# A second feed-forward over tokens sorted by expert, instead of all tokens through all experts

## The reference

```python
gates = softmax(x @ Wg)                       # x: 2048 tokens x 128; 8 experts
top_g, top_i = top_k(gates, 2)                # two experts a token
top_g = top_g / top_g.sum(-1, keepdims=True)
w = zeros(2048, 8).at[arange(2048)[:, None], top_i].add(top_g)
gate_h = silu(einsum('td,edf->etf', x, W1))   # 128 -> 256, for each expert
up = einsum('td,edf->etf', x, W3)
y = einsum('etf,efd->etd', gate_h * up, W2)   # 256 -> 128
out = einsum('te,etd->td', w, y)
x = layernorm(x + out)
```

## Time and profile before

| | |
|---|---|
| Median of 3 runs | 1080.46 us |
| Lowest and highest of the runs | 1079.54 and 1086.42 us |
| Span of the profiled execution (first to last instruction) | 1083.5 us |
| Time of the profiled execution around its span | not listed |
| PE busy | 961.3 us, 89% |
| DVE busy | 749.5 us, 69% |
| ACT busy | 562.8 us, 52% |
| POOL busy | 354.1 us, 33% |

### The profile page before, as it was taken

The page is one execution under the profiler, slowest core; times in us unless marked ns, Lnnn a source line. Parts: engine busy times, 40 slices in busy tenths (PEclk is TensorE's granted clock), DMA queues, the critical chain, the costliest instruction groups (busy, mean ns, idle before and its releaser), DMA issues.

```text
span 1083.5 us, 17979 instructions
## 1 busy us (share of the span) xinstructions
PE 961.3 (89%) x6128; PEld 464.6 (43%) x6135; DVE 749.5 (69%) x1554; ACT 562.8 (52%) x621; POOL 354.1 (33%) x744
## 2 busy tenths in 40 slices
PE   5799999999999875799857889999999889999996
PEld 3222223223223543599724333333333335666664
DVE  7689999999997687244445977777778225654456
ACT  4479889888987322122216035455655665322232
POOL 2164345345335300478815013333333431000000
PEclk9599999999999998899955689999999989999999
DMA  5201101100200412267535221122201300001001
GB/s 199 98 2 44 45 1 44 44 24 19 83 1 2 137 29 54 61 160 189 97 88 199 94 90 46 50 86 90 73 17 44 104 2 1 1 15 44 1 1 40
DMA packets 49837, 65.45 MB, mean 60 GB/s; under 512 B 7800, under 2 KB 37848, under 8 KB 46296
## 3 DMA queue, kind: packets, MB, share of 16 engines
q1 hardware_dynamic: 43280, 58.63, 17.4%
q0 software_dynamic: 5632, 4.46, 2.9%
q10 hardware_dynamic: 864, 1.57, 0.4%
HBM read 51.74 MB, written 12.91 MB: 60 GB/s over the span
## 4 chain that ended last, share of the span: by engine, by line
PE 62%; DVE 23%; issue 7%; ACT 4%; DMA 2%; POOL 1%; DVEq 0%; SPq 0%; ACTq 0%
PE causal_ps L1243 10%; PE acc_ps L769 9%; DVE mx L518 6%; PE acc_ps L1111 6%; PE tail_ps L1057 5%; PE tail_ps L1258 5%; DVE R L1609 4%; PE causal_ps L1094 4%; PE causal_ps L967 3%; DVE tails L1615 3%; PE causal_ps L731 3%; PE tail_ps L967 2%; PE acc_ps L977 2%; PE causal_ps L742 2%; ACT EX L1476 2%
## 5 line engine op out<-in xcount | busy, mean ns | idle before, releaser
L1476 ACT ACTIVATE EX<-causal_ps 128x1024 f32<-128x1024 f32 (+1 forms) x160 | 147.0, 938 | 146.7 <-PE causal_ps L1094 145.5
L518 DVE TENSOR_REDUCE mx<-tail_ps 128x1 f32<-128x512 f32 x266 | 157.4, 633 | 39.2 <-PE tail_ps L1060 21.4
L1335 ACT ACTIVATE R<-R 128x2048 f32<-128x2048 f32 (+1 forms) x80 | 134.7, 1737 | 0.5 <-DVE R L1609 0.5
L1243 PE MATMUL causal_ps<-XT,w 128*128 128x512 f32 x256 | 115.7, 594 | 1.0 <-DVE hid_f L2033 1.0
L1094 PE MATMUL causal_ps<-QE,KE 75*128 75x512 bf16 (+3 forms) x384 | 102.6, 338 | 10.9 <-ACT EX L1476 5.5
L1057 PE MATMUL tail_ps<-KM,QM 72*128 72x512 bf16 (+1 forms) x320 | 102.2, 346 | 8.8 <-DVE mx L518 3.0
L1609 DVE TENSOR_SCALAR R<-causal_ps 128x1024 f32<-128x1024 f32 (+1 forms) x88 | 93.9, 1069 | 14.8 <-PE causal_ps L731 13.7
L1342 ACT ACTIVATE R<-R 128x1792 f32<-128x1792 f32 (+4 forms) x80 | 100.5, 1268 | 0.0
L1615 DVE TENSOR_REDUCE tails<-causal_ps 128x1 f32<-128x768 f32 (+4 forms) x96 | 92.8, 967 | 10.6 <-PE causal_ps L742 9.9
L1517 ACT ACTIVATE act_f<-causal_ps 128x512 f32<-128x512 f32 x64 | 38.1, 597 | 119.2 <-PE causal_ps L1243 119.2
L2262 POOL TENSOR_TENSOR pacer<-eps_ln 128x1 f32<-128x1 f32 x160 | 31.3, 196 | 210.0 <-ACT EX L1476 209.3
(11 more groups left out here) (306 smaller groups left out, 1618.9 us busy)
## 6 DMA issues: line engine op xcount, KB each, us to landing
QS<-q_parts SPq DMA_DIRECT2D x8, 576.0 KB
KS<-k_parts SPq DMA_DIRECT2D x24, 192.0 KB
QM<-q_parts SPq DMA_DIRECT2D x8, 576.0 KB
KM<-k_parts SPq DMA_DIRECT2D x24, 192.0 KB
QE<-q_parts SPq DMA_DIRECT2D x8, 576.0 KB
KE<-k_parts SPq DMA_DIRECT2D x24, 192.0 KB
wg<-in_wg_t SPq DMA_DIRECT2D x16, 256.0 KB
wu<-in_wu_t SPq DMA_DIRECT2D x16, 256.0 KB
```

The lines of the kernel that those rows point to most:

```text
L518: return reduce(mx[:, par, hh, o0:o0 + step * (cnt - 1) + 1:step], scores[:, 0:cnt * w].rearrange("p (c w) -> p c w", w=w), AX.X, op, **how)
L1243: mm = pe.matmul(banks[2 * m + o], w[:, k, m * P:(m + 1) * P], XT[:, n * BANK:(n + 1) * BANK], start=True, stop=True)
L1335: act.activation(R4[:, rp, h0:h0 + 2, 0:width], R1[:, rp, h0:h0 + 2, 0:width], ACT.Square).then_inc(squared, 1)
L1476: act.activation(EX[:, rp, hh, 0:width], causal_ps[hh % 2][:, 0:width], ACT.Exp, scale=float(D) ** -0.5).then_inc(exp_done, 1)
```

## The change

The second feed-forward takes only the pairs that count. A token occupies one row in a table for each of its two experts. The rows of an expert stand together and each expert's part is filled up to a multiple of 128 rows, so that a tile of 128 rows belongs to one expert. There are 23 tiles for a batch in all cases, 46 in total.

- `X` becomes 144 wide: after the 128 values of a token come its eight weights and eight row numbers, which say where the result of the pair goes.
- PE and DVE count the tokens of each expert (`count_half`, `total_experts`, `place`; `take_counts`, `pad_experts`, `take_slots`) and find for each pair its row in the table, and for each tile its expert.
- POOL scatters each batch's rows into `sorted_rows` in memory, 16 indirect transfers of 128 rows of 576 bytes a batch, without accumulation. SP has filled the table with zeros and with spare row numbers ahead, with four transfers in the second attention.
- SP loads each batch's table into `SR`, in three transfers (4, 7 and 12 tiles).
- For each tile, PE reads the number of its expert from SBUF into a register (`value_load`), and picks the weights by it. A tile has one matmul over 512 columns (w1 and w3 side by side), ACT's silu over 256 columns, DVE's product, two transposes of the product with a copy by ACT (`turn_hidden`, `copy_hidden`), two matmuls over 128 columns, and DVE's weighing.
- POOL scatters each tile's 128 rows into `y_rows`; SP loads both contributions of each token back, and DVE adds them (`add_both`) and normalises. This stands behind all the tiles on DVE.
- The weights of all eight experts are loaded at once in four transfers. The rest of the second attention and the routing of batch 1 stand ahead of the first tile, instead of between items. `route_half` of batch 0 stands one step earlier, and the last group's sums are transposed into another part of PSUM.
- POOL builds some 35 further constants, ahead of the first feed-forward's gathers.

The core of the diff:

```diff
             exp_quad(NQ - 1, NQ // 2 - 1, 1, False, turn_maxima=False, beside=[
-                [], [(0, lambda: turn_first(0))], [(0, lambda: turn_first(1))], [(0, lambda: route_half(0, 4))], []])
+                [], [(0, lambda: turn_first(0)), (0, lambda: turn_first(1))], [(0, lambda: route_half(0, 4))], [],
+                [(0, lambda: count_half(0, 5, 4))]])
...
+            def up(q):
+                b, j = divmod(q, LT)
+                i, k = divmod(j, CT)
+                pe.wait_ge(xt_sb, 3 * CH + NG * b + i + 1)
+                at_least(pe, f_hid, q - 1)
+                e = pe.value_load(expert_i[0:1, q:q + 1], min_val=0, max_val=E1 - 1)
+                pe.matmul(banks[q % 2], ST[:, (NG * b + i) % 2, k * P:(k + 1) * P],
+                          w13[:, bass.ds(e, 1), :].rearrange("p o f -> p (o f)"), start=True, stop=True).then_inc(f_up, 1)
+                return e
+            def turn_hidden(q):
+                pe.wait_ge(f_hid, q + 1)
+                at_least(pe, f_ht, q - 1)
+                for m in range(F1 // P):
+                    mm = pe.transpose(banks[2 + q % 2][:, m * P:(m + 1) * P], hid_f[:, q % 2, m * P:(m + 1) * P], ident[:, :])
+                mm.then_inc(f_hid_turned, 1)
+            def down(q, e):
+                pe.wait_ge(f_ht, q + 1)
+                at_least(pe, f_out, q)
+                for m in range(F1 // P):
+                    mm = pe.matmul(banks[4][:, 0:P], hid_t[:, q % 2, m * P:(m + 1) * P],
+                                   w2[:, bass.ds(e, 1), m, :].rearrange("p o d -> p (o d)"),
+                                   start=(m == 0), stop=(m == F1 // P - 1))
                 mm.then_inc(f_y, 1)
-            ffn_up(0, 0)
             run_all(exp_sums(NQ - 1, 1, NS - 1))
-            ffn_up(0, 1)
...
-            turn_exp(NQ - 1)
-            up(1)
+            total_experts(0, 5, 4)
+            turn_exp(NQ - 1, causal_ps[0])
+            place(0, 5, 4)
             turn_y(1, 2, 7)
             turn_y(1, 3, 6)
...
-            for p in range(6, len(FFN)):
-                down(p - 2)
-                up(p)
+            count_half(1, 6, 7)
+            total_experts(1, 6, 7)
+            place(1, 6, 7)
+            for q in range(NL + 2):
+                if q < NL:
+                    b, j = divmod(q, LT)
+                    if j == 0:
+                        pe.wait_ge(f_experts, b + 1)
+                        turn_sorted(b, 0)
+                    if j % CT == 2 and j // CT + 1 < NG:
+                        turn_sorted(b, j // CT + 1)
+                    expert_of[q] = up(q)
+                if 0 < q <= NL:
+                    turn_hidden(q - 1)
+                if q > 1:
+                    down(q - 2, expert_of.pop(q - 2))
...
@@ sync
             parts_stored(1, 1)
+            for b in range(B):
+                rows = sorted_rows[b].rearrange("(j p) w -> p j w", p=P)
+                sp.dma_start(rows[:, :, 0:P + E1], pad_zero[:, :].unsqueeze(1).broadcast_to([P, LT, P + E1])
+                             ).then_inc(zeros_out, 16)
+                sp.dma_start(rows[:, :, P + E1:XR], pad_to[:, b * LT:(b + 1) * LT, :]).then_inc(zeros_out, 16)
...
+            for b in range(B):
+                sp.wait_ge(f_sent[b], 16 * KT * TOP)
+                sp.dma_start(SR[:, b, 0:CT, :], sorted_rows[b][0:CT * P, :].rearrange("(j p) w -> p j w", p=P)
+                             ).then_inc(weights[b], 16)
+                for m in range(2):
+                    first, upto = (CT, LT // 2) if m == 0 else (LT // 2, LT)
+                    sp.dma_start(SR[:, b, first:upto, :], ...).then_inc(weights[2 + b], 16)
+            for b in range(B):
+                sp.wait_ge(scattered[b], 16 * (NH * E0 // 2 + LT))
+                for n in range(b * CH // B, (b + 1) * CH // B):
+                    for c, z in enumerate((Z, Z_two)):
+                        ...
@@ vector
+            for q in range(NL + 2):
+                if q < NL:
+                    b, j = divmod(q, LT)
+                    if j == 0:
+                        take_sorted(b, 0)
+                        weigh_slots(b)
+                    if j % CT == 2 and j // CT + 1 < NG:
+                        take_sorted(b, j // CT + 1)
+                    hidden(q)
+                if q > 1:
+                    weigh_out(q - 2)
+            for b in range(B):
+                chunks = range(b * CH // B, (b + 1) * CH // B)
+                for n in chunks:
+                    add_both(n)
+                for n in chunks:
+                    standardise(3, n)
...
@@ gpsimd
+            for b in range(B):
+                pool.wait_ge(f_slots, b + 1)
+                for t in range(KT):
+                    for c in range(TOP):
+                        pool.indirect_dma_start(out=sorted_rows[b], in_=X[:, b * KT + t, :], in_offset=None,
+                                                out_offset=...).then_inc(f_sent[b], 16)
+            for q in range(NL):
+                pool.wait_ge(f_out, q + 1)
+                pool.indirect_dma_start(out=y_rows, in_=y_out[:, q, :], in_offset=None,
+                                        out_offset=...).then_inc(scattered[q // LT], 16)
```

More of the change, by code:

```diff
@@ L171 @@
 FIRST_TURN = 8
[L174 to L177, removed]
+XR = P + 2 * E1
 XT2_BANK = (4, 5, 7, 6)
[L181 to L188, removed]
+LT = (TOP * T + E1 * (P - 1)) // P
+NL = B * LT
+GROUPS = [list(range(i, min(i + CT, LT))) for i in range(0, LT, CT)]
+NG = len(GROUPS)
+SLOTS = B * LT * P
+TE = KT * E1
 MASKS_AT = [sum(len(STEPS[i]) for i in range(s)) for s in range(NS + 1)]
@@ L490, in build @@
         f_exp = sem("f_exp")
-        f_win = [sem(f"f_win{i}") for i in range(HALF_E)]
+        f_sel = sem("f_sel")
+        f_counted = sem("f_counted")
+        f_counts = sem("f_counts")
+        f_total = sem("f_total")
+        f_padded = sem("f_padded")
+        f_placed = sem("f_placed")
+        f_slots = sem("f_slots")
+        f_experts = sem("f_experts")
+        f_sent = [sem(f"f_sent{b}") for b in range(B)]
+        f_weighed = sem("f_weighed")
         f_up = sem("f_up")
@@ L1247, in up, with count_half @@
[L1247 to L1252, removed]
-                pe.wait_ge(f_hid, KF * (p + 1))
-                if p >= 2:
-                    pe.wait_ge(f_acc, p - 1)
-                for i in range(CT):
-                    for m in range(KF):
-                        mm = pe.matmul(banks[4 + p % 2][:, i * P:(i + 1) * P], hid_f[:, p % 2, m, i * P:(i + 1) * P],
-                                       w2[:, e % HALF_E, m, :], start=(m == 0), stop=(m == KF - 1))
+            def count_half(b, at, small):
+                tiles = slice(b * KT, (b + 1) * KT)
+                chosen_of = sel[:, tiles, :].rearrange("p t e -> p (t e)")
+                pe.wait_ge(masks_ready, 5)
+                pe.wait_ge(f_sel, b + 1)
+                pe.matmul(banks[at][:, 0:TE], lower_t[:, :], chosen_of, start=True, stop=False)
+                pe.matmul(banks[small][0:TE, 0:1], chosen_of, ones1[:, :], start=True, stop=True).then_inc(f_counted, 1)
@@ L1275, in _ @@
             times_w(1, 3, 6)
-            down(1)
-            up(3)
-            down(2)
-            up(4)
             pe.wait_ge(z_sb, 2 * CH)
@@ L2035, in hidden @@
-            def hidden(p):
-                for m in range(KF):
-                    hidden1(p, m)
-            def add_up(p):
-                (e, n), q = FFN[p], ffn_before(p)
-                dve.wait_ge(f_y, p + 1)
-                if q is not None:
-                    dve.wait_ge(f_acc, q + 1)
-                for i in range(CT):
-                    t = n * CT + i
-                    before_it = X if q is None else Z
-                    ins = dve.scalar_tensor_tensor(Z[:, t, :], banks[4 + p % 2][:, i * P:(i + 1) * P], WT[:, e, t:t + 1],
-                                                   before_it[:, t, :], ALU.mult, ALU.add)
-                ins.then_inc(f_acc, 1)
-                if e == E1 - 1:
-                    dve.wait_ge(f_acc, p + 1)
-                    moments(3, n)
+                link(dve.tensor_tensor(X[:, tiles, P:P + E1], GW[:, tiles, :],
+                                       rowF[:, 1, tiles].unsqueeze(2).broadcast_to([P, KT, E1]), ALU.mult))
@@ new lines, in weigh_slots @@
+            def weigh_slots(b):
+                some = slice(b * LT, (b + 1) * LT)
+                dve.wait_ge(weights[b], 16 * (3 * E0 // 4 + 1))
+                dve.wait_ge(weights[2 + b], 16 * (3 * E0 // 4 + 2))
+                dve.wait_ge(f_experts, b + 1)
+                for c in range(2):
+                    ins = dve.tensor_tensor(chosen[:, c, :, :], SR[:, b, :, P + c * E1:P + (c + 1) * E1],
+                                            is_expert[:, b, :, :], ALU.mult)
+                link(ins)
+                link(dve.tensor_reduce(w_slot[:, b, :, :], chosen[:, :, :, :], AX.X, ALU.add))
+                dve.tensor_copy(to_row[:, some], w_slot[:, b, 1, :]).then_inc(f_weighed, 1)
```

(7 more changed lines are left out.)

358 lines of the change are left out of this document (224 added, 134 removed).

## The result

Median 1039.86 us (1035.40 to 1042.75, four runs) against 1080.66 us for the kernel before: ratio 0.961, 95% interval 0.9577 to 0.9643. The forecast was 1048 us. The profiled execution took 1042.75 us, span 1040.9 us; on the span the sum had said 1051.3.

A forecast was written before the change was run, and what follows sets the result against it. PE's array was taken to bound the dense feed-forward, 167 us of item matmuls. First product at 936, 45 tiles of 2.1 us to 1030.5, tail to 1051; 32.2 us off the median gives 1048 us, range 1028 to 1094, forecast's own 1039 to 1069.

The forecast's parts named there:

- A: Rival: PE's array binds the tiles and the register read is hidden; tile 1.7 to 1.9 us, 1030 to 1039 us; chance 0.17.
- short formula: The whole sum in short: span = 957 + 45 x (tile time), breaking even at 2.82 us a tile.
- Steps 1: Start, after the last sums' copy at 900.9: transposes, prefix matmul and DVE instructions, destination rows known at 905 us.
- step 2: POOL's 16 table scatters at 1.25 us (upper end 1.86), then 3.24 us to SP's next issue: 927 us.
- step 5: The 46 tiles: 1.69 us of PE array work each at full clock, 78 us against 167; ACT and DVE not the bound.
- step 7: Tail: last weighed output at 1033, DVE's adding and normalising 15.8 us, reload beneath the first two chunks, store 2.3 us: 1051.
- Step 4: Second batch's projection, normalisation and routing, meanwhile: 23 us from 907, so 930, six microseconds of slack against 936.
- step 3: Fetch of a batch's table, 7.4 us in three transfers, then DVE's weighing about 1 us: first product at 936 us.
- Step 6: PE's expert-number read each tile: 1.05 us with arithmetic, bounds nothing to 2.3 us; tile 2.1 us, 45 tiles 94.5 us.
- B: Rival: POOL binds in the table and output scatters at 1.86 us each; span 1066, time 1063 us; chance 0.07.
- C: Rival: PE's register read costs more than 2.0 us; tile 3.05 us or more, 1091 us or slower, 1105 at 2.3; chance 0.16.
- D: Rival: PE's clock stays at its lower level; at 1.2 GHz a tile's array work is 3.4 us, 1107 us; chance 0.06.

## Why the prediction was right, and where a size was off

**Luck in the total.** The sign and the mechanism were right, but the forecast tied 1039 to 1069 us to a tile of 1.9 to 2.55 us. The median, 1039.86, lies 0.9 us inside the first range; the tile, 1.81 us, lies outside the second and inside A's (1.7 to 1.9). By the short formula a tile of 1.81 us makes a span of 1038.5 and a time of 1035 us. That the median is higher comes mostly from the start, 1.4 us later than the sum had it, and from the median lying 1.0 us below the profiled span, where the forecast took off 3.0.

**Steps 1 to 3, 5 and 7 stood.** The scatters that do not add cost 0.97 + 0.30 = 1.27 us, the gather's price that step 2 took; adding costs 1.87, its upper end. The array's 1.69 us a tile of step 5 measured 1.64. That the fill is covered was shown by doubling it. In the tail DVE worked without a break from 1023.26: the reload of the second batch, issued at 1026.08, lay beneath the first batch's two chunks, as step 7 said. The lock-out of POOL by DVE that the prediction spoke of did not show either: the 78 scatters took 0.97 us at the median and 1.16 at the longest. (The Trainium skill gives the figures 620 and 3100 ns on the page that the prediction names, "SBUF — State Buffer", but in the section "A bandwidth-pool intuition that's wrong (but worth ruling out)".) Whether any DVE work beside the gathers or the scatters was in such a mode no run shows, so the trace doesn't speak against the page, as the prediction had it.

**Step 4's slack was not there.** Routing ended at 932.1 us, 5.3 us before the first product, but behind it the list of the tiles' experts, the tokens' copy, the read, the first up at half clock and the silu follow one another, and the lines of the start show no wait among them for anything else. The step counted as free the time that these need. The six microseconds did no harm to the forecast, because the weighing of step 3 ended only 0.28 us before the product. So routing 2.3 us sooner gained nothing: it only exposed the other chain.

**Step 6 was mis-sized.** A read with its arithmetic is 0.60 to 0.65 us, not 1.05; it lies between the bounds kept. By the step's own formula, tile = max(1.69, 1.05 + 0.65) = 1.70. Measured is 1.81, so the formula is also too simple. With four reads the tile is 3.33 us, which leaves 0.7 to 0.9 us beside four reads of 0.60 to 0.65, and not 1.05. By the maximum, one read would then hide completely (0.9 + 0.65 is less than 1.64); it does not, because PE's stream comes to it late in every other tile; in half of these the token transposes fill the gap. What holds the stream there was not taken apart further; that moving the read cures it is shown.

**The rivals.** A was half right: the clock was full, the array close to its bound, the tile lies in its range, and 1039.86 lies 0.9 us above the 1039 given for it. But the read was not hidden: 9.5 us of the stretch went with it. B, C and D did not occur: POOL waited for weighed outputs, the read is under 2.0 us, the clock among the tiles was 1.00. C's side is real, though: with four reads, 2.4 to 2.6 us, the kernel took 1110.9 us against 1081.9 before, and C had said 1091 to 1105 for 2.0 to 2.3.

**What decided the sign** was a stretch of expert matmuls 88.1 us shorter, against 35.5 of later start and 10.0 of tail, and the margin in the tile: at 1.81 + 42.6 / 45 = 2.76 us the gain was gone.

## What to carry to other kernels

An instruction that an engine's own stream must finish before it can issue the next matmul is priced by where it stands: ahead of the waits it lay under the matmul before it and cost nothing, behind them 0.18 us a tile of its 0.65. Ask of a bare start which of its parallel chains is longest before shortening one: routing 2.3 us faster gained nothing beside an 8 us fetch. Saved array time arrives less what its removal uncovers, here 88.1 us less 45.5.

## What the runs showed of the hardware

- TENSOR_LOAD on PE's queue is recorded at 0.30 us, but reads behind one another start every 0.65 us.
- An indirect scatter of 128 rows costs POOL 0.97 us plain (rows of 512 and of 576 B) and 1.56 us adding (512 B), with 0.30 us between two that follow each other directly.
- In the kernel with idle matmuls PE's clock fell all the same: granted 1.00 from 900 to 915 us with PE 9.77 of 15 us busy, 0.66 from 915 to 935 with 14.75 of 20. The idle matmuls show the two levels: the six of 903.26 us took 1.47 us, 0.25 each; the eleven of 919.30 us took 4.50, 0.41 each.
